# Gated experts: the product of the two upward halves on VectorE straight from PSUM, and wider spacing for three blocks

## What is computed

```python
x = x + xattn_l(layernorm(x), ctx)      # layers 0, 1, 3: softmax; layer 2: sigmoid scores
x = x + ffn_l(layernorm(x))             # 8 experts
# layers 0, 1 and 3, one expert (layer 1 does the whole block twice):
h = silu(x @ W_first) * (x @ W_second)  # the two "upward halves"; layer 3 has biases
y = h @ W_down
# layer 2: gelu(x @ up.T) @ down.T, no gate
```

## Time and profile before

| | |
|---|---|
| timed runs | 4492.52, 4495.08 (median), 4500.36 us |
| the profiled execution | 4501.86 us, its span 4499.4 us |
| TensorE busy (matmul) | 85% of the span |
| ScalarE busy | 87% |
| VectorE busy | 64% |
| GpSimd busy | 18% |
| TensorE clock granted | 0.969 of full speed in the mean |

### The profile page before, as it was taken

The page is one execution under the profiler, slowest core; times in us unless marked ns, Lnnn a source line. Parts: engine busy times, 40 slices in busy tenths (PEclk is TensorE's granted clock), DMA queues, the critical chain, the costliest instruction groups (busy, mean ns, idle before and its releaser), DMA issues.

```text
span 4499.4 us, 69707 instructions
## 1 busy us (share of the span) xinstructions
PE 3846.1 (85%) x26742; PEld 881.9 (20%) x26742; DVE 2881.3 (64%) x5732; ACT 3897.7 (87%) x4328; POOL 832.1 (18%) x719
## 2 busy tenths in 40 slices
PE   5888888988889888898988999888888888888886
PEld 2122112111122221122212221111111111112112
DVE  2988888778987789877602332110685679877823
ACT  3589999899988899889899899989987889988994
POOL 4010000530025300252512111111001110044002
PEclk8599999999999999999999999999999999999998
DMA  4221001100021110111102221110001000010001
GB/s 125 74 60 36 14 13 30 33 17 12 12 60 35 34 36 12 36 39 30 37 16 60 69 71 27 39 38 21 14 19 40 27 12 12 13 42 27 5 1 50
DMA packets 124482, 151.31 MB, mean 34 GB/s; under 512 B 29272, under 2 KB 76384, under 8 KB 124080
## 3 DMA queue, kind: packets, MB, share of 16 engines
q1 hardware_dynamic: 122640, 145.53, 12.0%
q10 hardware_dynamic: 1504, 1.28, 0.2%
HBM read 123.21 MB, written 23.51 MB: 33 GB/s over the span
## 4 chain that ended last, share of the span: by engine, by line
PE 49%; ACT 26%; DVE 13%; issue 6%; DMA 1%; POOL 0%; SPq 0%; ACTq 0%; POOLq 0%; DVEq 0%
PE av L861 20%; ACT prob L1020 17%; DVE mpart L1131 10%; PE scores L851 7%; PE side L882 5%; ACT above L1028 5%; PE scores L959 4%; PE side L977 4%; PE side L959 2%; DVE above L1135 2%; PE scores L873 1%; ACT ag L1071 1%; ACT tx L1062 1%; PE side L851 1%; PE scores L1001 0%
## 5 line engine op out<-in xcount | busy, mean ns | idle before, releaser
L1020 ACT ACTIVATE prob<-scores 128x1024 f32<-128x1024 f32 x2998 | 2947.6, 1036 | 277.1 <-PE scores L851 249.8
L1131 DVE TENSOR_REDUCE mpart<-side 128x1 f32<-128x512 f32 (+1 forms) x3456 | 2132.5, 657 | 634.9 <-PE side L882 622.3
L861 PE MATMUL av<-prob,VA 128*9 128x512 f32 x6528 | 867.7, 604 | 40.5 <-ACT prob L1020 37.5
L861 PE MATMUL av<-prob,VB 128*9 128x512 f32 x6528 | 865.2, 602 | 18.7 <-ACT prob L1020 17.9
L851 PE MATMUL scores<-QP,KA 32*128 32x512 f16 x2996 | 562.3, 390 | 145.8 <-ACT above L1028 82.0
L851 PE MATMUL scores<-QP,KB 32*128 32x512 f16 x3000 | 554.4, 385 | 144.6 <-ACT above L1028 71.4
L882 PE MATMUL side<-KA,QP 32*128 32x512 f16 (+1 forms) x2112 | 623.4, 390 | 41.4 <-DVE mpart L1131 29.2
L882 PE MATMUL side<-KB,QP 32*128 32x512 f16 (+1 forms) x2112 | 578.7, 379 | 33.5 <-DVE mpart L1131 30.7
L1135 DVE CUSTOM_DVE_ANT_0 above<-side,above 128x512 f32<-128x512 f32 x768 | 516.2, 686 | 71.9 <-PE side L882 62.4
L1028 ACT ACTIVATE above<-scores 128x1024 f32<-128x1024 f32 x384 | 394.1, 1026 | 82.0 <-PE scores L873 46.2
L1020 ACT ACTIVATE prob<-side 128x1024 f32<-128x1024 f32 x266 | 288.4, 1084 | 24.3 <-PE scores L851 23.8
(11 more groups left out here) (190 smaller groups left out, 2711.1 us busy)
## 6 DMA issues: line engine op xcount, KB each, us to landing
cwb<-weights SPq DMA_DIRECT2D x80, 256.0 KB, 4.0
KA<-kstacks SPq DMA_DIRECT2D x384, 48.0 KB
KB<-kstacks SPq DMA_DIRECT2D x384, 48.0 KB
Fin<-in_Fin SPq DMA_DIRECT2D x64, 256.0 KB, 2.8
kstacks<-hi SPq DMA_DIRECT2D x112, 128.0 KB, 2.4
ctxc<-in_ctxT SPq DMA_DIRECT2D x36, 256.0 KB, 3.1
kstacks<-lo SPq DMA_DIRECT2D x56, 128.0 KB, 2.5
hT<-in_mask SPq DMA_DIRECT2D x16, 400.2 KB, 3.3
```

The lines of the kernel that those rows point to most:

```text
L861: last = pe.matmul(AV[ROWS * h:ROWS * h + VC, :], V[l % 2][:, kt, g * HG + h, :], prob[:, (e + h // 2) % RING, (h % 2) * QB:(h % 2) * QB + ...
L1020: act.activation(prob[:, e % RING, :], pair.rearrange("p a b -> p (a b)"), ACT.Exp if softmax(l) else ACT.Sigmoid, scale=SCALE).then_inc(s ...
L1131: dve.tensor_reduce(part, bank, AX.X, ALU.max).then_inc(sem["red"], 1)
```

## The change

The step `gc` goes away: ACT no longer copies the second upward product. The step `gatea` moves from POOL to DVE and reads the second upward product in its PSUM pair, with the copy of the first one in `ag` as the other operand. It has a gap of 1 tick, so it is due one tick behind the second `up`. The pair is now free when `gatea` is done (`last_use`). POOL's `gateb` waits for DVE's `gatea`. This holds for units 0, 1, 2 and 6; the units that are `by_dve` stay as they are. Apart from that PACE places the PE steps of the finish of units 0 and 6 at one in 2 key tiles and of unit 1 at one in 1.5; unit 2 stays at one in each key tile.

```diff
--- before.py
+++ after.py
@@ -169,7 +169,7 @@
         return "upc", key
     if j < FFN[l]["nk"]:
         return "ac", key
-    return "gateb" if by_dve(u, lp) and l == 3 else "gc", (u, lp, k, j - FFN[l]["nk"])
+    return ("gc" if u == 3 else "gateb" if by_dve(u, lp) else "gatea"), (u, lp, k, j - FFN[l]["nk"])
 
 
 def wide(p, kt):
@@ -354,8 +354,7 @@
             out.append((2, Step("DVE", "gatea", (u, lp, k, j))))
             out.append((0, Step("DVE", "gateb", (u, lp, k, j))))
         else:
-            out.append((0, Step("ACT", "gc", (u, lp, k, j))))
-            out.append((0, Step("POOL", "gatea", (u, lp, k, j))))
+            out.append((1, Step("DVE", "gatea", (u, lp, k, j))))
             out.append((0, Step("POOL", "gateb", (u, lp, k, j))))
         if l == 3:
             out.append((0, Step("POOL", "gatec", (u, lp, k, j))))
@@ -469,7 +468,7 @@
             ysum=0.7, upc=0.7)
 Q = 4 * KT
 
-PACE = {3: (1.3, True), 4: (1.5, True)}
+PACE = {0: (2.0,), 1: (1.5,), 6: (2.0,), 3: (1.3, True), 4: (1.5, True)}
 
 LEAD, END = 12, 3
 
@@ -1070,15 +1069,6 @@
                         own.wait_ge(*o.sem("gateb", u, lp, k - 1, j))
                     act.activation(ag[0:fs, ch % 2, 0, :], bank_of(o, "up", u, lp, k, j)[0:fs, :], ACT.Identity if l == 3 else ACT.Copy,
                                    bias=b1[:, k, j:j + 1] if l == 3 else 0.0).then_inc(sem["bgA"], 1)
-                elif s.what == "gc":
-                    u, lp, k, j = s.key
-                    l = unit(u)[0]
-                    fs, nk, ch = FFN[l]["fs"], FFN[l]["nk"], 2 * k + j
-                    own.wait_ge(*o.sem("up", u, lp, k, nk + j))
-                    if ch >= 2:
-                        own.wait_ge(*o.sem("gatea", u, lp, k - 1, j))
-                    act.activation(ag[0:fs, ch % 2, 1, :], bank_of(o, "up", u, lp, k, nk + j)[0:fs, :], ACT.Identity if l == 3 else ACT.Copy,
-                                   bias=b1[:, k, nk + j:nk + j + 1] if l == 3 else 0.0).then_inc(sem["bgA"], 1)
                 elif s.what == "upc":
                     u, lp, k, j = s.key
                     own.wait_ge(*o.sem("up", u, lp, k, j))
@@ -1283,6 +1273,16 @@
                     l = unit(u)[0]
                     fs, ch = FFN[l]["fs"], 2 * k + j
                     a = ag[0:fs, ch % 2, 0, :]
+                    if not by_dve(u, lp):
+                        nk = FFN[l]["nk"]
+                        g = bank_of(o, "up", u, lp, k, nk + j)[0:fs, :]
+                        own.wait_ge(*o.sem("ac", u, lp, k, j))
+                        own.wait_ge(*o.sem("up", u, lp, k, nk + j))
+                        if l == 3:
+                            dve.scalar_tensor_tensor(a, g, b1[:, k, nk + j:nk + j + 1], a, ALU.add, ALU.mult).then_inc(sem["bgV"], 1)
+                        else:
+                            dve.tensor_tensor(a, g, a, ALU.mult).then_inc(sem["bgV"], 1)
+                        continue
                     own.wait_ge(*o.sem("tanh", u, lp, k, j))
                     own.wait_ge(*o.sem("ac", u, lp, k, j))
                     if ch >= 2:
@@ -1422,13 +1422,6 @@
                     if k >= 2:
                         own.wait_ge(*o.sem("up", u, lp, k - 2, 3))
                     pool.tensor_tensor(xk[:, k % 2, :], xnT[:], cwb[:, k % 2, :], ALU.mult).then_inc(sem["bgG"], 1)
-                elif s.what == "gatea":
-                    u, lp, k, j = s.key
-                    fs, ch = FFN[unit(u)[0]]["fs"], 2 * k + j
-                    a, g = ag[0:fs, ch % 2, 0, :], ag[0:fs, ch % 2, 1, :]
-                    own.wait_ge(*o.sem("ac", u, lp, k, j))
-                    own.wait_ge(*o.sem("gc", u, lp, k, j))
-                    pool.tensor_tensor(a, a, g, ALU.mult).then_inc(sem["bgG"], 1)
                 elif s.what == "gateb":
                     u, lp, k, j = s.key
                     fs, ch = FFN[unit(u)[0]]["fs"], 2 * k + j
@@ -1437,6 +1430,7 @@
                     pool.tensor_scalar(t, t, 1.0, None, ALU.add).then_inc(sem["bgG"], 1)
                     if ch >= H_RING:
                         own.wait_ge(*o.sem("down", u, lp, k - 2, j))
+                    own.wait_ge(*o.sem("gatea", u, lp, k, j))
                     pool.wait_ge(sem["bgG"], o.before("gateb", u, lp, k, j) + 1)
                     pool.tensor_tensor(hT[0:fs, ch % H_RING, :], t, ag[0:fs, ch % 2, 0, :], ALU.mult).then_inc(sem["bgG"], 1)
                 elif s.what == "gatec":
```

## The result

The changed kernel takes 4578.8 us in the median (4571.0 to 4587.0) against 4497.3 us before (the median over all its runs beside it). The ratio is 1.0182 with a 95% interval of 1.0162 to 1.0203: 81 us slower, where 4540 (43 more) was forecast and 4590 was the upper end. The profiled execution has a span of 4569.4 us, 70 more than before; it was the fastest of the four, so the profile shows less than the median does.

The account below looks back on a forecast made before the run. The prediction took the loop of PE score, ACT exp and pair release as tight, with no engine full. It summed +69 (wait) − 25 (ACT) + 0 (placement) + 0 (POOL, DVE) = +44, median 4540 us, range 4455 to 4590.

Parts of the forecast that it names:

- the slower rival: Whole kernel: no relief from ACT, sparse placement costs 13, DVE's queue 12, wait 69: +94, 4589 us; chance 0.17.
- Part 5, the new wait: PE's next score waits for DVE's product, queued behind reductions, to free the pair: 80 places, 0.86 us each, +69 us.
- The lower end: Of the new wait: 30% of 69, +21 us, if PE's slack in the tiles between takes the rest.
- Part 2, ACT's relief: ACT loses 80 copies, 49.1 us; half taken as gain, −25 us, with ends at 0 and −49.
- The draw between 48.6 and 49.1 of 54.5 us: ACT's and PE's busy times in the dense 17-tile stretch with experts, the reason for counting half of ACT's relief.
- the loop of two pairs: PE score, ACT exp, release of the pair, next score: looks one tile ahead, so quiet tiles don't make up delays.
- Part 1, the spacing: Sparser expert steps in units 0, 1 and 6: taken as 0, at best 20 us won, at worst 13 lost.
- the quiet 41.4 of rows 3: Time in us of a 17-key-tile stretch without background work; with experts 54.5, 0.82 us a step.
- Part 4, DVE's work: 80 new products on DVE, 56 us, beside experts where it is 72% busy: taken as 0, at most +12 us.
- the contention that the prediction weighed: A VectorE instruction with two SBUF inputs contends with a GpSimd one reading SBUF; could delay products up to 1.05 us.
- the second kind: VectorE instructions with a single SBUF input, said not to contend with GpSimd; the new product was placed here.
- Part 3, POOL: GpSimd, 18% busy, loses 80 products of 1.272 us: worth 0, as its work is covered.

Follow-up runs that it names:

- the longer wait: The changed kernel with the old PACE line, plus an extra VectorE copy of the same bank before each product: 4653.5 us, ratio 1.0339.
- spacing alone: The kernel before with only the new PACE line for units 0, 1 and 6, copy and GpSimd's product as before: 4516.3 us, ratio 1.0048.
- the product alone: The changed kernel with the old PACE line, so product on VectorE, no copy, one PE step in each key tile: 4570.7 us, ratio 1.016.
- the side bank with the same spacing: The changed kernel, its new PACE line included, with the second upward product in a single bank and not in a pair: 4488.8 us, ratio 0.9981.
- work alone: The kernel before with ACT's copy kept and only the product moved from GpSimd to VectorE, reading two SBUF copies: 4508.0 us, ratio 1.002.

## Why the prediction came out as it did

The direction, the mechanism and its place were right, and the time lies in the range. But the range is that of all the rivals: 4579 is outside the forecast's own 4515 to 4565 and stands 10 us from the slower rival's 4589, which had a chance of 0.17. The forecast of +43 was about half of the measured +81; two terms were mis-sized, and a third was put at nothing and measured 9.

*Part 5, the new wait, +69*: right, and some 8 to 11 too high. The waits of PE for the product add up to 61 us in the changed kernel. Taking them away by one tick gave 58 us (48 to 67). The lower end, a loop that makes up for 70% of it, is out: the longer wait was paid in full and more. The reading of the order of steps, not of busy shares, is what carried.

*Part 2, ACT's relief, −25*: this is the step that failed. It was "half, as the shares are a draw". It measured about 0: −3 us (−7 to +1) for 30 us of relief without the wait, and with the wait the copy could be put back for nothing that shows. The draw between 48.6 and 49.1 of 54.5 us was no draw. The prediction itself had said that no engine is full there and that the loop of two pairs sets the pace; from that it follows that a relief that doesn't shorten the loop is worth nothing. In the one place read closely, ACT's copy lay behind the upward product, while PE was busy with scores and the av anyway.

*Part 1, the spacing, 0*: mis-sized, its worst end of +13 was the better value. Alone it cost 13 to 30 us by the times and 8 by the units' part of the profile, in the change about 10, which is not clear of noise. The stretch of 17 tiles in the changed kernel, with 18 matmuls of upward and downward products (9 steps), takes

```profile
848.50:900.30 51.80, 43.38 (x298) 9.38 (x298) 38.50 (x74) 41.80 (x49) 12.36 (x10) 1.00 0.09 24
```

which is 10.4 us over the quiet 41.4 of rows 3. Four stalls of 0.86 make 3.4 of these and leave 7.0 for 9 steps, 0.78 each. So in this stretch a step costs the same as in a dense one, as the forecast had it. The clock may be where the spacing's price arises: the runs of spacing alone and of the change have a granted clock of 0.966 in the mean, those of the kernel before and of the product alone 0.969. The kernel before took 4489.7 us in a run at 0.972 and 4507.1 in one at 0.966, 2.9 us for each 0.001, so 0.003 would be worth some 9 us; this is an estimate. Against it, the side bank with the same spacing has 0.969. It was not tested.

*Part 4, DVE's work, 0*: measured +9 (5 to 13), inside its bounds of 0 to 12. The product itself took 0.68 us, as L1337 did, and 0.74 with the bias, as L1301. One reading of the rows was wrong: L1290, with two SBUF operands, has not one long case but 14 of 48, 0.91 to 1.73 us. In the trace of the kernel before each of these 14 overlaps a GpSimd instruction that reads SBUF (L1424, L1447 or L1482), and the 30 that overlap none take the usual 0.68 us. Two of the lines:

```profile
2441.89 1.27 POOL L1424 TENSOR_TENSOR tx<-xnT,cwb 128x512 f32<-128x512 f32 x1
2442.02 1.68 DVE L1290 SCALAR_TENSOR_TENSOR ag<-tx,ag 128x512 f32<-128x512 f32 x1
```

L1337, with one operand in PSUM, overlaps GpSimd's work six times and stays at 675 to 678 ns. This bears out the contention that the prediction weighed, and the second kind for L1337. The new product couldn't show it: no product overlaps any GpSimd instruction, neither in the changed kernel (64 of L1284) nor in work alone, whose 80 have two SBUF operands and take 676 to 694 ns.

*Part 3, POOL*: nothing speaks against it. In the changed kernel the downward products wait for GpSimd once, for 1.3 us, as before. No run took GpSimd's product away alone.

The measured terms: 61 (PE's waits in the trace) + 0 + 10 + 9 = 80, against 81. The agreement is closer than the terms are known, each to some 5 to 10 us. The errors hardly cancelled: 25 that did not come back, and 10 and 9 that were put at 0, less the 8 by which the wait was too dear. Of the rivals, the slowest (+94) was nearest; its reason, no relief, was right.

## What to carry to other kernels

Before a read of PSUM moves to another engine, ask who waits for the bank to be free, and what is queued in front of the read on the new engine; two short reductions of 0.65 us in front of it made an 0.68 us instruction cost 0.9 us, eighty times. Where a ring of two buffers sets the pace, as here, taking work from the busiest engine can be worth nothing, and taking one tenant out of the ring (here 80 upward products, −23 us with no instruction changed) is worth more than moving arithmetic. Try such an order edit and such a bank edit alone before judging the instruction.

## What the runs showed of the hardware

*The clock.* With longer holes in PE's work PE itself ran slower. With 47 us more waiting for the product, spread over 80 places, the granted clock of the profiled execution went from 0.969 to 0.958, and the same matmuls of units 1 to 3 had 34 us more of busy time. Between the levels of 1.2 and 2.4 GHz a mean of 0.958 over 4652 us is 391 us at the lower one, and 0.969 over 4569 us is 283: this is an estimate from the means.

The changed kernel has a trace of the same. Its profiled execution has 0.969, as before, but that was the fastest run; the other three have 0.964 to 0.966. And the 0.969 hides two opposite moves. The four units with the products are at 1.00, 0.99, 0.99 and 0.98, where they were at 1.00, 1.00, 1.00 and 0.99, and PE is busy 26.5 us longer there; the stretch without products between them went the other way. That stretch, before and then changed:

```profile
2370.10:3898.40 1528.30, 1330.71 (x9198) 294.72 (x9201) 735.20 (x1429) 1368.09 (x1473) 194.86 (x157) 0.96 0.12 34
```

```profile
2430.50:3954.00 1523.50, 1324.45 (x9198) 294.12 (x9200) 734.52 (x1429) 1367.36 (x1472) 194.02 (x157) 0.97 0.12 34
```

So a part of the 77.7 us in the four units may be the clock's and not the wait's own; no run holds the clock fixed.

*VectorE and GpSimd.* A VectorE instruction with two SBUF operands took 0.91 to 1.73 us in place of 0.68 in 14 of the 18 cases in which it overlapped a GpSimd instruction, and in none of the other 30 (L1290, kernel before). L1303, which also reads two operands from SBUF, took 1.58 to 1.60 us in place of 0.69 in the three cases of overlap. With one operand in PSUM (L1337) six overlaps changed nothing.
